# Routed experts' loop: the next tile's rows are turned ahead of the up product and of its GELU, Pool's high part reads one tensor, and table words are 16 bits wide

## The reference, cut to what matters

```
xt   = h.reshape(rows, 512)                       # 2048 rows
probs = softmax(xt @ W_router)                    # 16 experts
top_v, top_i = top_k(probs, 2)
rt_mid = gelu(xt @ Wrt_up[e])                     # 512 -> 256, for each chosen expert e
routed = sum_e gate[e] * (rt_mid @ Wrt_down[e])   # 256 -> 512
out  = x + gb * (shared experts + routed)
```

## Time and profile before

| what | value |
|---|---|
| median of the three runs | 942.76 us (938.45, 942.76, 944.33) |
| span of the profiled execution, first to last instruction | 937.6 us |
| the profiled execution's own time | not listed apart; the fastest run shown is 938.45 us, 0.8 us over the span |
| PE busy over the span | 892.2 us (95%) |
| DVE / ACT / POOL busy | 529.4 / 383.2 / 381.2 us |
| granted TensorE clock, mean | 0.984 of full speed |
| expert loop, up product of tile 0 to up product of tile 40 | from about 728 to 879 us of the span |

### The profile page before, as it was taken

The page is one execution under the profiler, slowest core; times in us unless marked ns, Lnnn a source line. Parts: engine busy times, 40 slices in busy tenths (PEclk is TensorE's granted clock), DMA queues, the critical chain, the costliest instruction groups (busy, mean ns, idle before and its releaser), DMA issues.

```text
span 937.6 us, 13563 instructions
## 1 busy us (share of the span) xinstructions
PE 892.2 (95%) x4264; PEld 719.0 (77%) x4265; DVE 529.4 (56%) x999; ACT 383.2 (41%) x632; POOL 381.2 (41%) x282
## 2 busy tenths in 40 slices
PE   7899869999998999999999999999999999999996
PEld 2457658878776888788888888888877888888875
DVE  5897797988667111274327432742486444444488
ACT  2557565573736533322232223215452333333352
POOL 2332200100022446416301630167815599998573
PEclk9899989999998999999999999999999999999999
DMA  9548578566046426876212521267353789876887
GB/s 357 192 129 255 199 231 256 158 203 203 23 157 209 144 97 206 243 239 209 91 34 72 198 90 34 87 203 282 114 157 124 247 248 278 279 247 223 260 252 194
DMA packets 121824, 174.03 MB, mean 186 GB/s; under 512 B 8216, under 2 KB 69656, under 8 KB 118704
## 3 DMA queue, kind: packets, MB, share of 16 engines
q1 hardware_dynamic: 58896, 111.55, 34.9%
q0 software_dynamic: 9216, 34.61, 12.1%
q10 hardware_dynamic: 53664, 27.26, 9.9%
HBM read 97.58 MB, written 75.81 MB: 185 GB/s over the span
## 4 chain that ended last, share of the span: by engine, by line
PE 71%; DVE 12%; DMA 5%; issue 4%; ACT 3%; POOL 3%; SPq 1%; DVEq 0%; ACTq 0%
PE kk_ps L425 6%; PE kk_ps L427 6%; PE kk_ps L426 6%; PE kv_ps L425 6%; PE kv_ps L427 6%; PE kv_ps L426 6%; PE mm_ps L425 4%; PE mm_ps L426 4%; PE mm_ps L427 4%; PE up_ps L425 3%; PE dn_ps L425 3%; PE dn_ps L427 3%; PE dn_ps L426 3%; PE up_ps L426 2%; PE up_ps L427 2%
## 5 line engine op out<-in xcount | busy, mean ns | idle before, releaser
L1563 DVE TENSOR_TENSOR silu<-kk_ps,silu 128x512 fp32r<-128x512 f32 x64 | 44.2, 691 | 196.5 <-ACT silu L2229 196.2
L2225 ACT ACTIVATE kk_ps<-kk_ps 128x512 f32<-128x512 f32 x64 | 37.2, 582 | 206.5 <-PE kk_ps L427 206.5
L425 PE MATMUL kk_ps<-xk,cm_w 128*128 128x512 f32 x256 | 100.9, 394 | 2.3 <-DVE xk L1608 2.3
L425 PE MATMUL kv_ps<-cm_w,silu 128*128 128x512 f32 x256 | 100.6, 393 | 0.0
L427 PE MATMUL kk_ps<-xk,cm_w 128*128 128x512 f32 x256 | 99.8, 390 | 0.0
L427 PE MATMUL kv_ps<-cm_w,silu 128*128 128x512 f32 x256 | 99.7, 390 | 0.0
L426 PE MATMUL kk_ps<-xk,cm_w 128*128 128x512 f32 x256 | 99.6, 389 | 0.0
L426 PE MATMUL kv_ps<-cm_w,silu 128*128 128x512 f32 x256 | 99.6, 389 | 0.0
L2393 POOL TENSOR_TENSOR cm_w<-stage,cm_w 128x1024 fp32r<-128x1024 f32 x16 | 38.7, 2423 | 90.5 <-ACT cm_w L2013 74.7
L2400 POOL TENSOR_TENSOR rs<-mv,neghalf 128x4 f32<-128x4 f32 (+2 forms) x13 | 13.8, 1065 | 144.1 <-DVE mv L1274 144.0
L1890 DVE TENSOR_TENSOR xsT<-xs_ps,xsT 128x512 fp32r<-128x512 f32 x42 | 28.9, 691 | 73.9 <-ACT xsT L2310 73.9
(11 more groups left out here) (297 smaller groups left out, 2361.6 us busy)
## 6 DMA issues: line engine op xcount, KB each, us to landing
xs_s<-zero ACTq DMA_DIRECT2D x13, 1024.0 KB, 6.1
ys_s<-zero ACTq DMA_DIRECT2D x13, 1024.0 KB, 6.3
xsb<-xs_s SPq DMA_DIRECT2D x44, 256.0 KB, 3.8
ys_s<-ysb SPq DMA_DIRECT2D x41, 256.0 KB, 3.4
ex_raw<-in_wex POOLq DMA_DIRECT2D x9, 1024.0 KB, 6.3
stage<-in_wcm SPq DMA_DIRECT2D x16, 512.0 KB, 3.7
wmod<-in_wmod SPq DMA_DIRECT2D x6, 1024.0 KB, 11.8
ex_raw<-in_wex SPq DMA_DIRECT2D x6, 1024.0 KB, 8.0
```

What stands on the lines that cost most here:

```text
L425: pe.matmul(out, lhs[0], rhs[0], start=first, stop=False)
L1563: dve.tensor_tensor(silu[:, g % NSILU, 1, :], kk_ps[g % 2][:, :], silu[:, g % NSILU, 0, :].bitcast(F32), ALU.subtract).then_inc(s_silo, 1)
L2225: act.activation(kk_ps[g % 2][:, :], kk_ps[g % 2][:, :], ACT.Silu).then_inc(s_silu, 1)
```

## The change

Four edits, all in the routed experts:

1. PE: in both halves of the pair, `turn_x` (for tile t+1) comes ahead of `up` (of tile t) and no longer behind it.
2. ACT: the high part of the rows of tile t+1 comes ahead of the GELU of tile t. DVE's and SP's orders stay as they are.
3. POOL: the high part of an expert's weights is made by `tensor_scalar` (times 1.0) from the raw weights alone, and no longer by `tensor_tensor` with a broadcast column of zeros.
4. The table `tab` is of 16-bit unsigned words, and no longer of 32-bit integers. PE and SP read their registers from it as before.

```diff
+U16 = mybir.dt.uint16
...
-        tab = sbuf(top, "tab", [1, 2, NSX], I32)
+        tab = sbuf(top, "tab", [1, 2, NSX], U16)
...
             def pair(i, w0, w1):
+                turn_x(0, i * 16 + 32)
                 up(w1, slot_of(w1), 1, i * 2 + 2)
-                turn_x(0, i * 16 + 32)
                 down(slot_of(w0), 0, i * 2 + 1, i * 2 + 1)
                 w2 = word_of(i * 2 + 2)
                 turn_m(1, i * 2 + 2)
+                turn_x(1, i * 16 + 32)
                 up(w2, slot_of(w2), 0, i * 2 + 3)
-                turn_x(1, i * 16 + 32)
                 down(slot_of(w1), 1, i * 2 + 2, i * 2 + 2)
                 w3 = word_of(i * 2 + 3)
                 turn_m(0, i * 2 + 3)
...
             with act.Fori(0, pairs) as i:
+                turned_hi(0, i * 2 + 3)
                 gelu4(1, i * 2 + 2)
-                turned_hi(0, i * 2 + 3)
                 turned_mid_hi(1, i * 2 + 2)
+                turned_hi(1, i * 2 + 4)
                 gelu4(0, i * 2 + 3)
-                turned_hi(1, i * 2 + 4)
                 turned_mid_hi(0, i * 2 + 3)
...
-                pool.tensor_tensor(hi, raw_of(e), zero[:, 0:1].to_broadcast([P, UNIT]), ALU.add).then_inc(s_exd, 1)
+                pool.tensor_scalar(hi, raw_of(e), 1.0, None, ALU.mult).then_inc(s_exd, 1)
```

## The result

The changed kernel takes 957.87 us (median of 4 runs, 955.2 to 962.35), the kernel before 943.55 us in the same comparison: a ratio of 1.0174, 95% interval 1.0138 to 1.0209. It is 1.7% slower, beyond the upper end of the range that was forecast. The profiled execution took 955.2 us, its span is 953.3 us.

The account below looks back on a forecast made before the run. It took the loop's chain PE, ACT, DVE, PE to bound the kernel. Terms -11.2 - 1.7 + 14 + 1 gave +2 us on a median of 942.8, so 945 us, range 933 to 952.

Parts of the forecast that it names:

- POOL's high part: Making an expert's high part on POOL: 2.7 us instead of 3.71, bounds 3.7 and 1.8, hidden unless PE waits for weights.
- The turn and ACT's order: Expert loop: the up product's wait for DVE's low part goes, 3.46 us a tile, -11.2 us; GELU moved at no cost.
- SP's queue: Row loads queued behind a store start 2.4 us after the turn, leaving 4.5 us to land: +14 us of stalls.
- my sum of +2 us: All terms together, -11.2 - 1.7 + 14 + 1, for the whole kernel against before.
- The word's read: PE's read of a table word between down product and middle's turn may last 0.9 us: +1 us (0 to 2).
- 16-bit words: Register reads by PE and SP from the narrower table: taken as 0, bounds +-1 us.
- The third rival: The 0.23 us idle is PE's sequencer and stays, period 3.74 us: +8, 951 us; chance 0.06.
- The first: Rival: row landings fit the new spacing, stalls cost 0 to 6 us: -5 to -12, about 934 us; chance 0.28.
- the second: Rival: slower through the load behind the store, +12 at most, 951 to 955 us; chance 0.12.
- its ring: A late store holds DVE's copy, the next store, the row load behind it in SP's queue, then PE, feeding itself.

Follow-up runs that it names:

- the last kernel with tensor_copy: Turn ahead with SP's row loads one store earlier, DVE's copy out later and tensor_copy on POOL, against the kernel before: ratio 0.9978 (0.9954 to 1.0002).

## Why the prediction was wrong

**The step that failed** is "POOL's high part": "2.7 us (bounds: 3.7, no gain, and 1.8, twice the step)", and with it "With my forecast of no faster PE it is worth nothing". It took 5.4 to 5.9 us, above the upper bound. I reasoned from the number of tensors, and took it for granted that the new form could be no slower. No row showed a tensor_scalar on POOL, so the upper bound had no reason behind it. With the earlier trace rows the price would have been easy: nine splits at 1.8 us more against 1.9 us of slack are 14.5 us. The experiment that changes only this and the words' width shows 16.8 us (1.0179), and the changed kernel with tensor_copy in that one place is back at 1.0022, inside the range.

The Trainium skill, "GPSIMD Engine Reference", in Engine selection (under When to use GPSIMD), calls one-input operations roughly line-rate and two-input ones slower. The copy agrees (1.91 us for 2,048 elements a partition, against 4.6 for two whole tensors), tensor_scalar does not: at 5.38 us it is slower than the two-tensor subtraction of 4.6 us, and above the 3.07 us that this page's best case for a plain loop gave in the prediction. The measurement decides.

**The turn and ACT's order** were right: the chain GELU, high part, low part was the wait, the periods are 3.47 us instead of 3.74, and in the kernel with ACT's order left alone the up product again starts 0.23 us behind DVE's low part, in periods of 3.57. The gain is 39 x 0.27 = 10.5 us in the loop, against 11.2.

**SP's queue** was right as a mechanism and nearly in size: 14 us were forecast, 17.0 measured (15.4 without POOL's new form). Two things in it were off. The load comes 2.9 us and not 2.4 after the turn in one half of the pair. And the late landings were put down to weights alone, where up to 800 us most of the waits went with the adds, DMAs of 256 KB that add DRAM rows into a buffer in SBUF. So that the size came out nearly right is partly luck. For the turn ahead and the words my sum of +2 us stands against +4.4 (1.0047).

**The word's read** cost nothing: "Estimate +1 us" can't be seen, and all ordinary periods are 3.47. **16-bit words**: 0, right.

**The clock** was in no term. The wait of 6.8 us brought the 1.2 GHz level for the next tile, 2.2 us here, and the three waits of the kernel with tensor_scalar alone cost 4 us so. Waits for rows can bring it too. In the kernel with the turn ahead and the words:

```profile
843.06 0.65 PEld L1176 LDWEIGHTS xs_ps<-ident,xsb 128*128 128x128 f32 x4 [2.99 <-DMA xsb<-xs_s]
843.69 0.34 PEld L426 LDWEIGHTS up_ps<-ex_w,xsT 128*128 128x128 f32 x1
...
848.47 0.19 PEld L426 LDWEIGHTS up_ps<-ex_w,xsT 128*128 128x128 f32 x1
```

That tile took 4.78 us, 1.3 more than 3.47, and the granted clock was 0.50 from 844 to 846 us:

```profile
844.00:846.00 2.00, 2.00 (x11) 2.00 (x11) 0.69 (x1) 0.60 (x1) 1.00 (x3) 0.50 0.65 213
```

The same followed waits of 2.2 us (turn ahead with tensor_copy), 2.3 and 2.5 (turn ahead on PE only) and 2.8 us (the last kernel with tensor_copy). It did not follow the longest wait for rows of the changed kernel. Its row in the timeline, and the busy time and the clock of the stretch behind it:

```profile
779.60 0.42 PEld L1176 LDWEIGHTS xs_ps<-ident,xsb 128*128 128x128 f32 x4 [3.52 <-DMA xsb<-xs_s]
...
779.00:783.00 4.00, 3.40 (x23) 3.09 (x24) 0.69 (x1) 0.98 (x2) 3.37 (x2) 1.00 0.61 222
```

Here the next period is 3.48 us. So between 2.2 and 3.5 us the length of a wait alone does not tell whether the clock falls; what else decides is open. In the trace of the turn ahead and the words 1.3 of the 4.3 us that its loop lost are the clock's.

The third rival (the wait is PE's sequencer) fell. The first, that the landings fit, fell too. Of the second its ring was there (13.4 us of copies out waiting for a store in the kernel with the turn ahead), but the whole kernel lost 4.4 us and not 8 to 12.

What stays open: why tensor_scalar is slow on POOL. The rounding to fp32r alone is not it, as the copy rounds too in 1.91 us; whether it is the multiplication or the constant was not tried. And how much of the late rows is due to the adds' bytes, how much to their being adds and not plain copies.

## What to carry to other kernels

An operation whose form no row of the trace shows has no upper bound from its neighbours: time it alone before it goes into a chain with 1.9 us of slack, and try the copy first where a copy will do. When an engine's step is moved ahead, look in the queues of the engines that were not touched: here SP's order, right for the old loop, put every load behind a store, and took back what the turn had gained. Costs that fall on one engine's waits in one stretch need not add: in the loop 15.5 and 4.3 us gave 13.8. And look at the granted clock behind each wait of PE: the tile behind it can cost 1.3 to 2.2 us more.

## What the runs showed of the hardware

- POOL, 128x2048 f32 into fp32r: tensor_copy 1.91 us, tensor_tensor with a broadcast column 3.6, with two whole tensors 4.6, tensor_scalar with a constant 5.38. In the changed kernel the tensor_scalar took 5.80 to 5.87 us in the four rounds in which two DMA issues of POOL's own went just ahead.
- SP reads a 16-bit word as fast as a 32-bit one (medians of 0.265 us with the words alone and 0.271 before), PE too (0.55 and 0.57 us).
- TensorE's granted clock was 0.50 when PE started again after 6.8 us without a matmul, and for about 5 us more. It was also at 0.50 in the tile behind eight shorter waits for rows or weights, of 2.2 to 5.0 us, and stayed at 1.00 through others of up to 3.5 us.
- Row loads of 256 KB landed in 2.4 us at the shortest and 8.1 at the longest. Issued one store earlier they took as long (medians of 3.4 against 3.5 us); without the eight adds of 256 KB the median was 2.8 us.
